# Graph attention: POOL weighs the gathered source rows, two windows ahead, between its gathers

## The reference, cut to what matters

```
edge_features = concat([h[dst], h[src] * dir_w, dir_w, feat])      # h: the initial rows, dir_w: one number per edge
edge_attr = edge_features @ W_ee + b_ee
for i in range(3):
    q, k, v = projections of h_cur;  e = edge_attr @ We[i] + be[i]
    alpha = (q[dst] * (k[src] + e)).sum(-1) / sqrt(128);  w = softmax of alpha over the edges of one dst
    out = segment_sum((v[src] + e) * w, dst), mean over 3 heads, plus a skip product
    h_cur = relu(out + residual)
```

## Time and profile before

| | |
|---|---|
| median of 3 runs | 4387.33 us (4382.59 to 4400.81) |
| the profiled execution | 4409.32 us, its span from first to last instruction 4407.5 us |
| mean granted TensorE clock | 0.908 of full speed |
| busy share of the span | PE 79%, DVE 41%, POOL 41%, ACT 32% |
| GpSimd instructions, the gathers of this attention (L2291) | 1344 of 1907, 1351.5 us |
| the product on VectorE (L2713) | 225 instructions, 212.4 us |

### The profile page before, as it was taken

The page is one execution under the profiler, slowest core; times in us unless marked ns, Lnnn a source line. Parts: engine busy times, 40 slices in busy tenths (PEclk is TensorE's granted clock), DMA queues, the critical chain, the costliest instruction groups (busy, mean ns, idle before and its releaser), DMA issues. The chain is left out here.

```text
span 4407.5 us, 82939 instructions
## 1 busy us (share of the span) xinstructions
PE 3495.3 (79%) x22381; PEld 2087.8 (47%) x22381; DVE 1826.6 (41%) x5369; ACT 1429.6 (32%) x3483; POOL 1819.9 (41%) x1907
## 2 busy tenths in 40 slices
PE   4999999948757878776677777857777678999998
PEld 2666656635534444444344444433334344555564
DVE  4665656647533333333333333323333333244222
ACT  3454545532533333332222223312222223122112
POOL 2444445520146655654565666456655640000000
PEclk8999999979879999998898888878888889999999
DMA  5666666548454554545566666566566645443223
GB/s 137 178 182 180 178 181 168 167 89 254 119 143 130 136 139 132 141 130 140 154 167 170 179 177 170 150 166 167 160 165 162 164 117 177 168 173 131 73 89 129
DMA packets 716528, 675.29 MB, mean 153 GB/s; under 512 B 382359, under 2 KB 542945, under 8 KB 716117
## 3 DMA queue, kind: packets, MB, share of 16 engines
q1 hardware_dynamic: 622598, 466.26, 36.6%
q0 software_dynamic: 77008, 200.24, 17.3%
q10 hardware_dynamic: 16768, 6.91, 0.6%
HBM read 530.84 MB, written 142.28 MB: 153 GB/s over the span
## 5 line engine op out<-in xcount | busy, mean ns | idle before, releaser
L2291 POOL DMA_INDIRECT l_y<-s_lrows,l_src x1344 | 1351.5, 1006 | 991.7 <-issue 346.9
L2371 PE MATMUL ps<-l_y,aw_pT 128*63 128x277 f32 x2700 | 445.8, 475 | 287.7 <-ACT aw_pT L2589 283.9
L3402 PE MATMUL ps<-nl_adj,nl_table 126*128 126x504 bf16 (+1 forms) x3150 | 631.4, 357 | 2.3 <-DVE nl_table L3637 2.3
L996 POOL DMA_INDIRECT em_gs<-s_rows,em_idx x400 | 400.5, 1001 | 247.2 <-issue 86.0
L2355 PE MATMUL ps<-aw_yT,aw_qt 128*63 128x384 f32 x1800 | 370.9, 523 | 130.3 <-DMA aw_yT<-s_dxT 61.1
L3402 PEld LDWEIGHTS ps<-nl_adj,nl_table 126*128 126x128 bf16 x3150 | 301.8, 96 | 298.9 <-issue 5.6
L2748 DVE COPY aw_axd<-ps 128x252 f32<-128x252 f32 x225 | 94.6, 421 | 798.0 <-remote 390.0
L2371 PEld LDWEIGHTS ps<-l_y,aw_pT 128*63 128x63 f32 x2700 | 198.5, 156 | 461.9 <-ACT aw_pT L2589 316.7
L2328 PE MATMUL ps<-ident,l_y 128*128 128x128 f32 x1800 | 282.5, 293 | 154.8 <-issue 78.7
L2589 ACT ACTIVATE aw_pT<-ps 128x381 f32<-128x381 f32 x225 | 109.7, 487 | 770.1 <-remote 572.6
L2575 ACT ACTIVATE aw_yT<-ps 128x512 f32<-128x512 f32 (+1 forms) x525 | 261.4, 536 | 258.0 <-remote 111.8
(11 more groups left out here) (381 smaller groups left out, 5921.0 us busy)
## 6 DMA issues: line engine op xcount, KB each, us to landing
nl_adj<-s_adj SPq DMA_DIRECT2D x20, 3100.8 KB
aw_yT<-s_dxT SPq DMA_DIRECT2D x150, 384.0 KB
aw_geoS<-s_geoS SPq DMA_DIRECT2D x450, 94.5 KB
nl_adj<-s_adj SPq DMA_DIRECT2D x15, 2325.6 KB
ws_msg<-s_msg SPq DMA_DIRECT2D x75, 384.0 KB, 3.8
s_dxT<-aw_yT SPq DMA_DIRECT2D x75, 384.0 KB
aw_qt<-s_qt SPq DMA_DIRECT2D x225, 126.0 KB
s_msg<-em_msg SPq DMA_DIRECT2D x100, 256.0 KB
```

What stands on the lines that cost most here:

```text
L996: pool.indirect_dma_start(out=gs[:, u, j, :], out_offset=None, in_=d["rows0"], in_offset=bass.IndirectOffsetOnAxis(ap=slot[:, u, 2 * j:2 * ...
L2291: pool.indirect_dma_start(out=y[:, u, j, 0:W], out_offset=None, in_=table, in_offset=bass.IndirectOffsetOnAxis(ap=src[:, u, j:j + 1], axis ...
L2371: m = nc.tensor.matmul(k.ps[64 * v:64 * v + HW, SUM, 0:SW], pT[:, SLOT[u], j, 64 * v:64 * v + HW], y[:, u, v * TH + j, 0:SW], start=j == 0 ...
L3402: m = nc.tensor.matmul(k.ps[:, bank(i, p), 0:cols * WN], source[:, p, q, b, :], adj[:, a % 2, 0:cols, b * WN:(b + 1) * WN], start=b == 0 a ...
```

## The change

The product leaves VectorE. POOL does it with six small `tensor_scalar` instructions for each window (128 x 128 each, one for each `j`), for the window two before the one that it is gathering: two of them behind the second, two behind the fourth and two behind the sixth gather. Ahead of the first pair POOL waits until the rows and the edge data of that window have landed (`weigh_starts`). The two gates are taken out. A semaphore `weighed` tells that all six are done; in layer 0 PE waits for it where it waited for VectorE, in layers 1 and 2 a wait for it is new in `sums`. The mask on VectorE takes over the wait for `summed`. Two set-up semaphores are merged into others (`query_mixed` into `mixed`), with the same order of work.

```diff
-    ready = steps("ready", ["DX", "SEL", "OFF"], U, NW)
+    ready = steps("ready", ["SEL", "OFF"], U, NW)
+    weighed = steps("weighed", ["DX"], U, NW)
...
     def gpsimd(pool):
-        def gather(w, u):
+        def weigh_starts(w, u, i):
+            pool.wait_ge(rows_in[u], (i + 1) * 16 * T + rows_base[u])
+            pool.sem_inc(hop["pool"], 1)
+            pool.wait_ge(in_[u], (i + 1) * 96 + in_base)
+            pool.sem_inc(hop["pool"], 1)
+
+        def weigh(u, j):
+            m = nc.gpsimd.tensor_scalar(y[:, u, j, D:2 * D], y[:, u, j, W - D:W], y[:, u, j, G0:G0 + 1], None, ALU.mult)
+            if j == T - 1:
+                m.then_inc(weighed.sem, 1)
+
+        def gather(w, u, i):
             if started(w, U):
                 pool.wait_ge(summed.sem, summed.of(w - U, "AG"))
...
             for j in range(T):
-                if started(w, U) and j == 2:
-                    pool.wait_ge(scored.sem, scored.of(w - 3, "S"))
-                    pool.sem_inc(hop["pool"], 1)
-                if started(w, U) and j == 4:
-                    pool.wait_ge(turned.sem, turned.of(w - 2, "T1"))
-                    pool.sem_inc(hop["pool"], 1)
                 pool.indirect_dma_start(out=y[:, u, j, 0:W], out_offset=None, in_=table,
                                         in_offset=bass.IndirectOffsetOnAxis(ap=src[:, u, j:j + 1], axis=0)
                                         ).then_inc(rows_in[u], 16)
+                if started(w, 2):
+                    if j == 1:
+                        weigh_starts(w - 2, (u - 2) % U, i if u >= 2 else i - 1)
+                    if j % 2 == 1:
+                        for n in range(j - 1, j + 1):
+                            weigh((u - 2) % U, n)
...
+        for u in (U - 2, U - 1):
+            weigh_starts(NW - U + u, u, NW // U - 1)
+            for j in range(T):
+                weigh(u, j)
...
                 if l == 0 and n == 1:
-                    pe.wait_ge(ready.sem, ready.of(w, "DX"))
+                    pe.wait_ge(weighed.sem, weighed.of(w, "DX"))
...
         def sums(w, u):
             pe.wait_ge(pT_ok.sem, pT_ok.of(w, "P"))
             pe.wait_ge(agr_ok.sem, agr_ok.of(w - 1, "AG"))
+            if l:
+                pe.wait_ge(weighed.sem, weighed.of(w, "DX"))
...
-        def weigh(w, u, i):
-            dve.wait_ge(rows_in[u], (i + 1) * 16 * T + rows_base[u])
-            dve.wait_ge(in_[u], (i + 1) * 96 + in_base)
+        def mask(w, u):
+            s = ready.sem
             if started(w, U):
                 dve.wait_ge(summed.sem, summed.of(w - U, "AG"))
-            nc.vector.tensor_tensor(y[:, u, :, D:2 * D], y[:, u, :, W - D:W], bc(y[:, u, :, G0:G0 + 1], [128, T, D]),
-                                    ALU.mult).then_inc(ready.sem, 1)
```

More of the change, by code:

```diff
@@ L2138, in attention_windows @@
         xs = sb("xs", [D, CW])
-        w2_in, query_mixed, query_mixed_c = sem("w2_in"), sem("query_mixed"), sem("query_mixed_c")
+        w2_in = sem("w2_in")
         rows_out, qt_out, qs_out, next_src = sem("rows_out"), sem("qt_out"), sem("qs_out"), sem("next_src")
@@ L2297, in gpsimd @@
             before.rows_stored(pool)
+        weighed.prime(pool)
         for u in range(1 if before is None else 0, U):
-            gather(u, u)
+            gather(u, u, 0)
         with pool.Fori(1, NW // U) as i:
             for u in range(U):
-                gather(U * i + u, u)
+                gather(U * i + u, u, i)
+        for u in (U - 2, U - 1):
+            weigh_starts(NW - U + u, u, NW // U - 1)
+            for j in range(T):
+                weigh(u, j)
     def tensor(pe):
@@ L2465, in mix_queries @@
                                          start=True, stop=True)
-                m.then_inc(query_mixed, 1)
+                m.then_inc(mixed, 1)
             elif n == 1:
-                pe.wait_ge(query_mixed_c, 2)
+                pe.wait_ge(mixed_c, steps + 2)
                 for h in range(2):
                     m = nc.tensor.matmul(k.ps[:, 6 + h, 0:2 * D + GK], wqT[:, h * D:(h + 1) * D], kb[:, h, :], start=True, stop=True)
-                m.then_inc(query_mixed, 1)
+                m.then_inc(mixed, 1)
             else:
-                pe.wait_ge(query_mixed_c, 4)
+                pe.wait_ge(mixed_c, steps + 4)
                 nc.tensor.matmul(k.ps[:, 6, 0:2 * D + GK], wqT[:, 2 * D:3 * D], kb[:, 2, :], start=True, stop=True)
@@ L2511, in turn @@
                 if queries:
-                    pe.wait_ge(query_mixed_c, 7)
+                    pe.wait_ge(mixed_c, steps + 7)
                 pe.wait_ge(mixed_c, steps)
@@ L2768, in mix_queries @@
         def mix_queries(n):
-            dve.wait_ge(query_mixed, n + 1)
+            dve.wait_ge(mixed, n + 2)
             if n == 0:
-                nc.vector.tensor_copy(wqT[:, :], k.ps[:, 6, 0:H * D]).then_inc(query_mixed_c, 1)
+                nc.vector.tensor_copy(wqT[:, :], k.ps[:, 6, 0:H * D]).then_inc(mixed_c, 1)
                 nc.vector.tensor_copy(kb[:, :, D:2 * D + GK], k.ps[:, 7, 0:H * (D + GK)].rearrange("p (h f) -> p h f", h=H)
-                                      ).then_inc(query_mixed_c, 1)
+                                      ).then_inc(mixed_c, 1)
             elif n == 1:
                 for h in range(2):
-                    nc.vector.tensor_copy(abc[:, h, :], k.ps[:, 6 + h, 0:2 * D + GK]).then_inc(query_mixed_c, 1)
+                    nc.vector.tensor_copy(abc[:, h, :], k.ps[:, 6 + h, 0:2 * D + GK]).then_inc(mixed_c, 1)
             else:
-                nc.vector.tensor_copy(abc[:, 2, :], k.ps[:, 6, 0:2 * D + GK]).then_inc(query_mixed_c, 1)
+                nc.vector.tensor_copy(abc[:, 2, :], k.ps[:, 6, 0:2 * D + GK]).then_inc(mixed_c, 1)
                 bias_of = k.ps[:, 7, 0:3 * H].rearrange("p (h t) -> p h t", t=3)
-                nc.vector.tensor_copy(ab[:, :, 0:2], bias_of[:, :, 0:2]).then_inc(query_mixed_c, 1)
-                nc.vector.tensor_copy(ab[0:GK, :, 2:3], bias_of[0:GK, :, 2:3]).then_inc(query_mixed_c, 1)
+                nc.vector.tensor_copy(ab[:, :, 0:2], bias_of[:, :, 0:2]).then_inc(mixed_c, 1)
+                nc.vector.tensor_copy(ab[0:GK, :, 2:3], bias_of[0:GK, :, 2:3]).then_inc(mixed_c, 1)
         def split_geometry(c):
@@ L2805, in turn @@
             if not (isinstance(w, int) and w == NW - 1):
-                weigh(w + 1, (u + 1) % U, i if u < U - 1 else i + 1)
                 mask(w + 1, (u + 1) % U)
@@ L2837, in vector @@
             dve.sem_inc(indexed.sem, U)
-        weigh(0, 0, 0)
         mask(0, 0)
```

2 lines of the change are left out of this document (removed).

## The result

The change takes 5090.45 us (median of 4 runs, 5086.03 to 5097.53) against 4390.31 for the kernel before in the same runs: a ratio of 1.159, 95% interval 1.157 to 1.162. I had forecast a loss of 6.5%, 4675 us; it is 16%. The time lies inside the stated range of 4460 to 5150, near its upper end, and the loss is more than twice the one forecast.

A forecast was written before the change was run, and what follows sets the result against it. No engine was full; a loop of about 9.7 us, with PE's signals delayed by streaming gathers, bound the kernel. Layer 0 +297, layer 1 -27, starts and ends +15 gave +285: 4675 us, range 4460 to 5150.

The forecast's parts named there:

- The ring of layer 0: Layer 0: sums, gathers, POOL's products, features and sums again follow one another; 14.15 us a window against 10.08, +297 us.
- I take 0.30 each, nearest to the 128 x 128 row: POOL's price for each product, from a short 128 x 128 instruction 0.29 us long; 1.8 us a window, upper bound 0.5 each.
- starts and ends: At each layer's start and end, products queue behind gathers or follow them: some 5 us a layer, +15 us.
- I add 0.5 for a PE that may get a lower clock: Layer 0: 0.5 us a window added because PE now waits, raising 13.65 to 14.15.
- Layers 1 and 2: With the gates gone POOL's own round bounds them at 9.6 us a window; layer 1 wins 27 us, layer 2 nothing.
- The holding of PE's tellings: PE's signals arrive late while POOL's gathers stream; if this persists without gates, about 5290 (chance 0.10), partly 4800 to 5150 (0.18).
- E: POOL's products stretched by DVE's work beside them, 0.5 us each: 4930; shares a chance of 0.18 with the partial hold.
- Rival C: Products run while the gather ahead closes, POOL's round 7.7 us, layers 1 and 2 faster: 4305 to 4400, chance 0.09.
- D: A small loss: layer 0's POOL term near its lower bound, layers 1 and 2 slightly better: 4410 to 4560, chance 0.07.
- Free as said: Costs nothing: DVE's 212 us of lost work, PE's new wait in `sums`, merged set-up semaphores, the mask's wait for `summed`.

The follow-up runs named there:

- The halves: The changed kernel with each POOL product cut into two of 64 columns, twelve instead of six a window: 5409.74 us, 1.226 against the kernel before.

## Why the prediction was wrong, step by step

**The ring of layer 0: right in kind, too small by half.** Forecast 14.15 us a window, measured 17.73. By the timeline of the changed kernel: sums to first gather 0.97 (forecast 0.95); POOL 10.76 (9.0); product to features 0.06 (0.1); the sums 2.72 in the mean of the layer, 201.3 / 74 (1.62); and what is left for features and the work before the sums, 3.2 (0.58 and 1.4). That is 1.8 more for POOL and 2.3 more for PE, of which I had allowed 0.5.

**The step that failed first** is "I take 0.30 each, nearest to the 128 x 128 row". It is 0.60 to 0.63, twice that and above my upper bound of 0.5 for the instruction. POOL's part of the ring is 10.76, above its upper bound of 10.2, and the round is 10.95 against that bound's 10.8; gaps that shrink beside the products kept it so near. The row that I took was of the right shape and of another operation, and I counted a start-up as the whole. The halves show start-up and columns apart. By the price measured, the sum is 297 + 131 (layer 0) + 71 + 95 + 15, some 610, near 5000. Between the 285 us forecast and the 680 of the two profiled executions lie 395: by the windows this price is some 315 of them (128, 101 and 84 in the three layers), the term below some 140, and starts and ends take back 59.

**The second** is "I add 0.5 for a PE that may get a lower clock". It is a term of its own in a ring: PE waits 7.6 us for each window's products (548.5 / 72), gets 0.70 of its clock, and the work that stands in the ring is then longer. The run with added matmuls wins back 1.5 us a window, 115 us, of the 2.3. The other 0.8 was not taken apart.

**Layers 1 and 2: right in kind.** POOL's round bounds them, `sums` doesn't wait for the products, the gates cost nothing; 9.6 was forecast, 10.97 and 10.78 measured, by the same price.

**The holding of PE's tellings: right for the 4400 kind, and not one of my reasons told of the other.** I read the holding out of two timelines and gave its return 0.28, full and part together (the part shared with E). It did not come: three pairs of products of 1.19 us a window are pauses enough, and the maximum of layer 2 waited 45.5 us in all for PE and for nothing "remote". But I had taken the holding for a property of gathers; on the 3770 kind the same gathers hold nothing. Rival C, products in the gaps, falls: the gap before them shrinks from 0.30 to 0.03, yet a pair of products lasts 1.19. D falls with it. E named 0.5 a product and a time of 4930, for a reason (VectorE beside it) that the runs don't bear out: the halves put it down to start-up and columns, and the products take 0.63 us with VectorE's product gone.

**Free as said:** VectorE's lost work gave back 33 us of gather time (1351.5 to 1318.0), under the 80 allowed; merged semaphores and the mask's wait don't show. Starts and ends: I said +15 and they gave 44 back; why wasn't tried.

## What to carry to other kernels

Before work goes behind another engine's wait, follow what it feeds back to that wait: here a product that another engine could do as well ended up between one window's sums and the next, and it cost 6 us a window where its own time is 3.3. Price an instruction by two rows of its engine, one short and one long, so that start-up and columns come apart, and give the clock of an engine that will wait in a ring a term of its own. And before a wait that the profile calls "remote" is made part of an argument, measure the same kernel again at another time and place: the wait may be gone.

## What the runs showed of the hardware

The same program took 3770 us in some measurements and 4400 in others. Where it takes 4400, what PE tells other engines arrives late while POOL's gathers follow one another by 0.30 us, 12 us late in the rows above. Three POOL instructions of 0.24 to 0.31 us a window between the gathers don't help, one of 1.2 us does in part, and with three pairs of 1.2 us no such wait is left. A product of 128 columns on POOL takes 0.63 us, one of 64 columns 0.46. I have not found what sets the two kinds apart, the chip or something else. All twelve traces of the 4400 kind have "remote" waits, and the eight of the 3770 kind have not one, on any engine. In the four kernels that ran on both, the first maximum is 135 to 175 us earlier on the 3770 kind, while gathers alone take 952 ns on either kind. The edge network ahead of the attention gathers too; in it VectorE waits 182.7 us for "remote" in the change on the 4400 kind (54 times), and never on the 3770 kind.
